# The third difference ahead of the second eviction of h, and the second half of the gram rows ahead of the second mix

## What is computed

```
# layer 0, on a = groupnorm(x) as (8, 16384, 256)
attn = softmax(a^T a)                        # 256 x 256 for each image
x    = x + gamma * (a @ attn) + a
# layer 1, on g = groupnorm(x)
g    = (g - min(g)) / (max(g) - min(g) + 1e-7)            # over each image
log_m = [log(box_sum(g, k) + 1e-7) for k in (2, 4, 8, 16)]   # k x k windows
alpha = slope of log_m over log(k)           # least squares
excite = sigmoid(relu(mean(alpha) @ w1 + b1) @ w2 + b2)
sim  = cosine of (log_m - mean) and the fitted line - mean
out  = x + sim * sigmoid(batchnorm(alpha)) + (1 - sim) * g * excite
```

## Time and profile before

| | |
|---|---|
| median of three runs | 7060.63 us (7059.15 to 7066.81) |
| the profiled execution's own time | 7073.4 us |
| its span, first to last instruction | 7071.6 us |
| mean granted TensorE clock | 0.886 of full speed |
| VectorE busy | 5823.8 us (82%) |
| TensorE busy | 5245.1 us (74%) |
| ScalarE busy | 4867.7 us (69%) |
| GpSimd busy | 1535.4 us (22%) |
| DMA queue of the data | 50.8% of 16 engines' span |

### The profile page before, as it was taken

One profiled execution on the slowest core, in us unless ns is written; L12 is line 12 of the kernel. 1 busy time (PEld: TensorE's weight loads), 2 busy tenths in 40 slices (PEclk: granted clock), 3 DMA queues, 4 the chain that ended last, 5 costly groups with the idle time before them and its releaser, 6 DMA issues. The chain is left out here.

```text
span 7071.6 us, 107841 instructions
## 1 busy us (share of the span) xinstructions
PE 5245.1 (74%) x35320; PEld 4754.5 (67%) x35320; DVE 5823.8 (82%) x6709; ACT 4867.7 (69%) x5203; POOL 1535.4 (22%) x945
## 2 busy tenths in 40 slices
PE   7968885888858887688858888588876777466643
PEld 6767775777757776677757777577765666466642
DVE  1359997899969998699978999699987999699971
ACT  0128885788848877588857888488875888588861
POOL 0022222222132211321222212221213212322210
PEclk9989997999979998899979999799987999788875
DMA  3634443556535655465545655365653555344446
GB/s 114 195 116 152 145 142 122 176 196 211 190 128 201 204 190 174 147 211 196 199 146 169 203 201 199 118 204 194 207 175 128 187 175 176 124 149 150 152 149 231
DMA packets 837653, 1210.47 MB, mean 171 GB/s; under 512 B 34608, under 2 KB 690000, under 8 KB 821072
## 3 DMA queue, kind: packets, MB, share of 16 engines
q1 hardware_dynamic: 837456, 1208.16, 50.8%
HBM read 671.16 MB, written 536.87 MB: 171 GB/s over the span
## 5 line engine op out<-in xcount | busy, mean ns | idle before, releaser
L384 POOL TENSOR_TENSOR t<-t 128x1024 f32<-128x1024 f32 (+3 forms) x800 | 1340.0, 1688 | 4325.4 <-DVE logs L962 4282.8
L516 PE MATMUL even<-band,t 128*128 128x128 f32 x12288 | 1866.2, 283 | 459.6 <-ACT logs L692 286.5
L516 PEld LDWEIGHTS even<-band,t 128*128 128x128 f32 x12288 | 1618.5, 196 | 543.2 <-issue 443.0
L497 PE MATMUL h_ps<-mix,xt 128*128 128x256 f32 x4096 | 1206.9, 447 | 603.2 <-DVE mx L877 562.9
L497 PEld LDWEIGHTS h_ps<-mix,xt 128*128 128x128 f32 x4096 | 865.1, 222 | 785.5 <-issue 519.2
L692 ACT ACTIVATE logs<-even,col 128x1024 f32<-128x1024 f32 x512 | 569.1, 1111 | 430.8 <-PE even L516 430.1
L877 DVE CUSTOM_DVE_ANT_0 h_out<-h_ps,shift,mx 128x512 f32<-128x512 f32 x512 | 382.7, 747 | 574.2 <-PE h_ps L497 574.1
L518 PE MATMUL even<-band,t 128*128 128x128 f32 x4096 | 791.9, 275 | 0.0
L474 PE MATMUL g_ps<-xa 128*128 128x257 f32 x2048 | 623.8, 386 | 41.6 <-DMA xa<-in_x_dram 41.6
L533 PE MATMUL o_ps<-ident,pd 128*128 128x128 f32 x2048 | 386.6, 321 | 318.8 <-ACT o_sb L746 176.3
L518 PEld LDWEIGHTS even<-band,t 128*128 128x128 f32 x4096 | 621.9, 192 | 0.0
(11 more groups left out here) (184 smaller groups left out, 10433.0 us busy)
## 6 DMA issues: line engine op xcount, KB each, us to landing
xa<-in_x_dram SPq DMA_DIRECT2D x256, 512.0 KB, 5.4
xb<-in_x_dram SPq DMA_DIRECT2D x256, 512.0 KB, 6.2
h_scratch<-h_out SPq DMA_DIRECT2D x128, 1024.0 KB, 4.1
hr<-h_scratch SPq DMA_DIRECT2D x256, 512.0 KB, 5.8
p_scratch<-x1t SPq DMA_DIRECT2D x256, 512.0 KB, 2.7
q_scratch<-ut SPq DMA_DIRECT2D x256, 512.0 KB, 4.1
pd<-p_scratch SPq DMA_DIRECT2D x256, 512.0 KB, 6.1
qd<-q_scratch SPq DMA_DIRECT2D x256, 512.0 KB, 6.9
```

What stands on the lines that cost most here:

```text
L384: ins = g.tensor_tensor(dst[:, hf, d:d + n, :], src[:, hf, d:d + n, :], src[:, hf, e:e + n, :], ALU.add)
L497: ins = t.matmul(h_ps[:, r * C:(r + 1) * C], xt[:, q % 2, jh, r, :], mix[:, jh, :], start=(jh == 0), stop=(jh == 1))
L516: ins = t.matmul(o, src[:, hf, at, :], band[:, which, :], start=True, stop=(which < 3))
```

## The change

On VectorE `high_contrast` (L931) moves ahead of the second `copy_h`. On TensorE the second half of the gram rows moves from between box 1 and box 3 to just ahead of the second `mix_x`, behind the first `turn_back`. Nothing is added or taken away, and no semaphore changes.

```diff
@@ TensorE, half_chunk
                 if Cs:
                     box(u, k, hf, 2)
                     box(u, k, hf, 1)
-                if A:
-                    gram_rows(n, hf, 1)
                 if Cs:
                     box(u, k, hf, 3)
...
                     turn_x(nb, 2 * hf + 1)
                 if Ds:
                     turn_back(2 * nd + hf, hf, 0)
+                if A:
+                    gram_rows(n, hf, 1)
                 if Bs:
                     mix_x(nb, 2 * hf + 1)
@@ VectorE, half_chunk
                 if Cs:
                     low_contrasts(u, hf)
+                    high_contrast(u, hf)
                 if Bs:
                     copy_h(nb, k, 2 * hf + 1, first, None)
-                if Cs:
-                    high_contrast(u, hf)
                 if Bs:
                     min_h(i, k, hf)
```

## The result

| | before | after |
|---|---|---|
| median of the runs | 7063.72 us (4 runs, 7059.15 to 7075.69) | 6873.38 us (4 runs, 6868.03 to 6875.72) |
| span of the profiled execution | 7071.6 us | 6866.3 us |
| its mean granted TensorE clock | 0.886 | 0.916 |

The account below looks back on a forecast made before the run. VectorE's own 22.4 us per half chunk plus its wait for TensorE's second mix bound the kernel. 194.1 + 6.5 - 8 = 193 us off the profiled 7073.4 us gave a 6868 us median; range 6842 to 6930.

Parts of the forecast that it names:

- The bound: Stages 3 to 8: VectorE's own work of 22.4 us a half chunk, plus 1.24 us waiting for TensorE's second mix.
- Part 1: L931 ahead of the second eviction fills up to 1.22 us of each wait; alone 130 to 194 us, taken as 165.
- Part 2: Gram rows in TensorE's 2.70 us hole leave 1.2 us; clock stays 2.4 GHz, second mix takes 1.97 us, not 3.60.
- The hole ahead of box 3: TensorE idle where the gram rows stood: at most 1.48 us, too short to pull the clock down.
- the sum: Both moves remove the same wait: 194.1 us in stages 3 to 8 plus 6.5 in stage 2, less 8, is 193.
- Stage 8: No gram rows there, so the clock still falls and 0.3 x 25 = 8 us of waits stay.
- stage 1: Gram rows cover one wait for the copy of x and uncover another: at most 10 us either way, taken as 0.
- The rule on GpSimd's port: L939 starts 2.30 us behind GpSimd's adds; at most 1.4 us of margin goes, 0.9 us stay, so no collision.
- The clock still falling in every half chunk: Remaining gaps still pull TensorE's clock low, so only L931's move works: 150 us gain, 6911 us; chance 10%.
- The block holding the mix up: Gram rows, between release of `h_ps` and second mix, delay the mix at low clock: slower, 7097 us; chance 4%.
- Something else in the wait's place: GpSimd's adds collide with L939, or h rows from DRAM come late: gain used up, 7050 to 7070 us; chance 3%.

Follow-up runs that it names:

- two placements: Against the changed kernel: second half of the gram rows ahead of the first mix, 6894.31 us; both gram halves ahead of the second mix, 6912.42 us.

## Why the prediction was right

**The bound.** VectorE's own work and one wait for the second mix: right. In stages 3 to 7 no second eviction waits any more, second evictions come 22.3 us apart (median of each stage; 22.1 to 22.5 foretold), and taking 1.2 us out of VectorE's work took 194 us off the kernel.

**Part 1.** Foretold 165 us by itself, measured 168. The reasoning was only half right. I took L931 to cover 1.22 us of each wait and 29 us of the 194 to stay; taking 1.21 us off each wait of the kernel before would leave 24, and 11 stayed, 1.4 to 2.3 a stage. The mix was to be slow in as many half chunks as before, and it was so in 16 or 17 of 32 instead of 24 to 26. In the kernel before, the hole, the low stretch and VectorE's wait had kept each other going; without the wait, a slow mix shortens the next hole.

**Part 2.** The mix at full clock was right: 1.97 us for 1.97. The hole is 1.84 us in the half chunk shown and not the 1.2 I had. The holes of stage 5 repeat in a turn of four half chunks, 2.70, 2.90, 2.96 and 3.16 us before and 1.39, 1.59, 1.65 and 1.84 now: I had read the shortest kind of before, the half chunk shown is the longest kind, and the gram rows fill 1.31 us of each, not 1.48. So the hole came nearer to one with a low stretch behind it (1.9 us, with both gram halves ahead of the mix) than I thought. The hole ahead of box 3, at most 1.48 foretold, is 1.35, and no low stretch followed it. By the ratios TensorE's half alone gives 171 us, VectorE's half alone 168, both 193: they remove the same wait, as the sum had it.

**Stage 8.** I left 8 us of waits, 0.3 for each of 25; 2.0 stayed. Most of the waits were not that long: 1.21 us off each leaves 3.3 us. The rest is as in part 1, 18 slow mixes of 32 instead of 24.

**What the sum left out.** Three things, each small. A wait costs more than the gap that the trace shows: without it the next instruction starts 0.08 us before the last one ends (3003.85 to 3004.99 is 1.14 for an instruction of 1.22), so 26 waits are worth 2 us more a stage, 12 in all. L886 now waits for the eviction ahead of it, 0.11 us in 24 of the 32 half chunks, 2.5 us a stage, about 15 in all. And stage 1, foretold at 0, gave 2 us. The last L931 of each stage costs nothing and gains nothing, but it moves 1.1 us into the stretch between the evictions, so 8 of the 15.6 us outside are no gain. With it, stage 3 adds up: -34.0 - 2.1 + 2.5 + 1.1 = -32.5, and -32.7 was measured. The other 8 us outside I can't tell from their scatter (98.1 to 99.2 us after, 98.4 to 103.2 before).

So the profile moved by 205 us where I had 193, and the medians by 190: the profiled execution of before stood 10 us above its median, that of after 5 below. That the median came out within 6 us of the forecast is in part luck: the 12 us and the 15 us cancel, and what the profile fell by more than foretold is hidden by where the two profiled executions stood.

**The rule on GpSimd's port.** The adds after, and L939 of the same half chunk:

```profile
3002.21 5.17 POOL L384 TENSOR_TENSOR t<-t 128x256 f32<-128x256 f32 x4 [17.50 <-DVE logs L962]
```

They end at 3007.38, and L939, at 3008.35, starts 0.97 us later; 0.9 were foretold. In stages 3 to 8 none of the 192 L939 was held up: each took 1.22 or 1.23 us. What happens without the margin stands in stage 9, in the kernel before as in the changed one. It has no phase B, so no evictions stand between L962, which releases the adds, and L939. In the changed kernel:

```profile
6016.66 2.37 POOL L384 TENSOR_TENSOR t<-t 128x1024 f32<-128x1024 f32 x1
```

```profile
6017.60 2.52 DVE L939 TENSOR_TENSOR logs<-logs 128x1024 f32<-128x1024 f32 x1
```

The add ends at 6019.03, and L939 takes 2.52 us instead of 1.22, till 1.1 us behind that end. So it goes through stage 9: 1.57 to 3.07 us for L939, 2.50 in the median of 30. By the Trainium skill (SBUF, section "Who interferes with whom") a VectorE instruction with two inputs in SBUF and a GpSimd one that reads SBUF contend for one port pair, and one waits for the whole length of the other. This trace agrees. The rows of the prediction showed no collision because they were all of stages with phase B. In stages 3 to 8 the margin held, but whoever packs VectorE tighter still has less than 1 us of it.

**The rivals.** The clock still falling in every half chunk: no low stretch at all between the first and last eviction of stages 3 to 7. The block holding the mix up: it didn't; at twice its length it did in the first two half chunks of a stage and in stage 2, and nowhere else. Something else in the wait's place: nothing but the 0.11 us of L886.

## What to carry to other kernels

When one engine waits for another in every turn of a loop, look at what the late engine's clock was in that turn: behind a hole of 2.7 us the matmuls were slow, the other engine waited for them, and so the next hole was as long again. Then either fill the hole with work that has no fixed place, or give the waiting engine work that is ready, and expect each to bring nearly the whole gain and not the two together. Before a block is moved, look at the first turn and at the stages with less work: two placements that were the same in the steady loop, or within 1.6 us a stage, lost 22 and 40 us, most of it there.

## What was not expected of the hardware

Leaving out matmuls made the kernel 19 us slower (6891.5 us against 6872.5): the clock fell again (0.94 in stage 5) and the waits came back. And what the clock costs depends on who waits: while VectorE waited for the slow mix, 26 of 32 half chunks of stage 5 had one (clock 0.93); when it had other work to do instead, TensorE's lateness ate into the next hole, and 17 had one (0.96). Where nearly all holes stay at 2.7 to 3.2 us, as in stage 5 without the second half of the gram rows, 20 of 32 were slow at half chunks of 22.4 us, against 26 at 23.7. Why that is fewer no run here tells.
